# A two-layer graph network with a tensor product: node part by the tile, six gathered blocks, and another order of TensorE's work in each window

## The chip, the cores and the metric

The kernel runs on one core of one Trainium2 chip. The metric is the device time of that core in microseconds (us) from launch to end; less is better. The engines of the core are TensorE (PE; PEld is its weight load), VectorE (DVE), ScalarE (ACT), GpSimd (POOL) and SyncE (SP), each of which takes its own instructions in program order. They wait for one another through semaphores only.

## The reference

There are N = 6250 nodes with 512 features and E = 100,000 edges, sorted by destination. The destinations are drawn so that low node numbers receive far more edges than high ones. Written for what the change touches:

```python
edge_index = jnp.stack([src, dst])
h = jnp.maximum(_layernorm(x), 0)                       # 6250 x 512
# two graph layers; norm = dinv[row] * dinv[col], self loops added
h0 = layer_norm(h, g0, be0)
h  = relu(segment_sum(norm * (h0 @ W0)[row], col) + b0 + h0 @ lw0.T + lb0)
x_final = h
h1 = layer_norm(h, g1, be1)
h  = relu(segment_sum(norm * (h1 @ W1)[row], col) + b1 + h1 @ lw1.T + lb1)
x  = x + (x_final + h) @ pw.T + pb                      # x1
# tensor product on x1
h  = jnp.maximum(_layernorm(x), 0)
x0, x1 = lin(h, W_up0, W_up1)                           # 128 + 3 * 128 channels
t  = edge_attr_8                                        # E x 8
for W in (W_mlp1, W_mlp2, W_mlp3): t = 1.679177 * silu(t @ W / sqrt(W.shape[0]))
tpw = t @ W_mlp4 / 8                                    # E x 512
...                                                     # messages of x0, x1, tpw, edge_attr_4
x  = x + lin_out(segment_sum(messages, dst)) / 10
```

## The kernel before

**Tiles.** The nodes are 49 tiles of 128 rows (`NW = 49`), which are also the 49 windows of destinations of a graph layer. The edges are 784 tiles of 128 (`NT = 784`). A block is `BT = 4` edge tiles, so there are 196 blocks per layer.

**Setup.** TensorE sums the squares of the weights (line 1175), then counts edges per node by products of one-hots that VectorE makes (the histogram, line 1163). VectorE scales the weights by the squares' column norms. From the counts come the degrees, and from these each window's range of blocks.

**Node part.** For each tile: SP loads `x` (`load_x`), VectorE takes mean and variance, ScalarE and VectorE together form the first layernorm with its relu (`hrel`), then the second one (`tn`). POOL multiplies by `g0` and adds `be0` into `t32`. TensorE transposes (line 1188), ScalarE copies the transpose to `AT` (line 634), and TensorE multiplies by `W0` (line 1198) and `lw0` (line 1200). ScalarE and VectorE scale and split the product in a high and a low half (`tout`), which SP stores as a row of the table `tab_d`, and VectorE adds `b0` to the other product, which SP stores in `hl_d`. Each engine handles two tiles in turn: `norm_tiles` for tiles 2j and 2j+1, all steps of both, then `table_tiles` for the pair before. On TensorE it is `turn_tiles` for both tiles and then `project_tiles` for both. All buffers are double.

**Graph layers.** For each layer POOL gathers the table rows of the edges' sources, four indirect DMAs per block (line 549), into a ring of `NK = 4` blocks. The indices of the next block are copied ahead (line 557), and the wait for the data of the previous block, which signals `arrived`, stands after the third of the four gathers (lines 560 and 561). For each window VectorE makes one-hots of destination against node, one per visit (`onehots`, line 986). TensorE accumulates in bank 0: first the window's own rows (`tw`, line 1226, loaded by SP), then a visit (line 1233, eight matmuls) to each block that has edges of the window. A block that lies across a window boundary is visited by both windows. It is called the shared block here: the first visit of a window goes to the last block of the window before, which is still in the ring. There are 244 visits to 196 blocks in a layer. POOL may overwrite a ring slot once its block's last visit is over.

**The order of the work.** A window passes through several engines. Each engine has a list of stages with a distance d, and `peeled` runs for each w every stage of the list, in the order written, on window w - d:

```python
            with eng.Fori(depth + 1, NW) as w:
                for d, f in stages:
                    f(w - d)
```

In layer 0 the lists are

```python
peeled(ve, [(1, layer_out), (0, onehots), (2, low), (1, second_norm)])
peeled(pe, [(0, edge_sum), (1, turn), (1, dense)])
peeled(sp, [(0, load_self), (0, load_hl), (1, store_r), (2, store_tab), (2, store_hl)])
```

`layer_out(w)` (line 1010) reads bank 0 once the sum of window w is done, and frees it for window w + 1. `relu_r` makes `r`, `second_norm` with `std` and `scaled` the second layernorm in `t32`, `turn` transposes it, `copy_at` copies the transpose, `dense` multiplies by `W1` and `lw1` (lines 1266 and 1268), and `high` and `low` split the result for the table of layer 1. In layer 1 the rest of a window is `turn_xs`, `copy_xT`, `project` (line 1282), `residual`, `relu_h`, `turn_h` (line 1291), `copy_hT`, `up` and `up_out` (which SP stores, `store_up`). Beside it the radial MLP runs over two groups of 512 edges per window, which belong to no window: `load_ef`, `layer1`, `act1`, `layer2`, `act2`, `layer3`, `act3`, `store_hid` (line 424). `layer1` and `layer3` share banks 4 and 5, so that `layer1(w)` waits for `act3(w - 3)`, and `act3(w)` waits until the store of `w - 1` has landed. SP's list there is

```python
peeled(sp, [(0, load_ef), (0, load_self), (3, store_up), (0, load_hl), (4, store_hid), (0, load_r0),
            (1, load_x), (2, store_x1)])
```

The tensor product that follows gathers rows of the up table for each edge, forms the messages and scatters them.

## Time and profile before

| what | value |
|---|---|
| median of the runs | 6345.55 us (3 runs: 6323.8, 6345.55, 6354.23) |
| profiled execution | 6386.15 us, span 6383.9 us |
| mean granted clock of TensorE | 0.897 |
| busy: PE, PEld | 4974.6 us (78%), 2304.6 us |
| busy: DVE, ACT, POOL | 2858.4 us (45%), 2315.3 us (36%), 2736.9 us (43%) |
| setup | 0 to 170.5 us |
| node part | 170.5 to 797.8 us |
| layer 0 | 804.8 to 2139.5 us |
| layer 1 | 2139.5 to about 3920 us |
| tensor product | about 3920 to 6383.9 us |

The times are those of one profiled execution. A stage ends where the next one's first instructions stand. The busy share is an average over stages with different limits, so the stages have to be read by themselves. A granted clock of 1.0 is TensorE's full speed.

### The profile page before, as it was taken

The numbers are of one execution on the slowest core, as the hardware profiler recorded it, in microseconds if no ns is written. First come the engines' busy times: TensorE is split into PE (matmuls) and PEld (weight loads), VectorE is DVE, ScalarE is ACT, GpSimd is POOL, SyncE is SP. The second block draws the span as 40 slices with busy tenths as digits, with TensorE's granted clock in tenths as the row PEclk, the third lists the DMA queues.
The fourth block names the chain that finished last, engine by engine and source line by source line (L and its number), as shares of the span: only waits on it lengthen the run. The fifth ranks groups of instructions, "written<-read, shape, count | busy, mean of one in ns | idle before, by whom it ended". The sixth has DMA issues, their size and how long they took to land.

```text
span 6383.9 us, 104141 instructions
## 1 busy us (share of the span) xinstructions
PE 4974.6 (78%) x16990; PEld 2304.6 (36%) x17137; DVE 2858.4 (45%) x8231; ACT 2315.3 (36%) x6178; POOL 2736.9 (43%) x3492
## 2 busy tenths in 40 slices
PE   6566646667888556667677777999999999999998
PEld 4233312223333212223333333444444444444444
DVE  6322211233344211212222224777777777777776
ACT  0222200011111001122333335666666666666665
POOL 0211166666665565544433332444443333333332
PEclk6788867789999768888898898999999999999999
DMA  2111166667766565566655553444444434343333
GB/s 74 56 59 62 57 178 189 204 204 219 222 215 220 155 185 177 179 182 180 181 177 171 172 177 117 120 115 117 118 121 117 117 113 116 116 119 114 116 115 99
DMA packets 433670, 916.78 MB, mean 144 GB/s; under 512 B 63093, under 2 KB 170869, under 8 KB 433510
## 3 DMA queue, kind: packets, MB, share of 16 engines
q0 software_dynamic: 195840, 641.89, 34.6%
q1 hardware_dynamic: 237798, 274.56, 13.2%
q8 instruction: 9, 0.15, 0.0%
q14 instruction: 23, 0.19, 0.0%
HBM read 787.79 MB, written 128.41 MB: 144 GB/s over the span
## 4 chain that ended last, share of the span: by engine, by line
PE 35%; issue 21%; ACT 10%; DVE 9%; DVEq 7%; ACTq 4%; DMA 4%; POOL 4%; another core or an unknown queue 3%; POOLq 2%; SPq 1%
PE bank L1233 8%; PE bank L1282 4%; PE bank L1198 4%; ACT dense_w L765 4%; POOL ring L549 3%; PE bank L1363 3%; PE bank L1266 3%; PE bank L1200 3%; DVEq L1081 2%; ACT hB L754 2%; PE bank L1268 2%; DVE hA L1089 2%; DMA tw<-tab_d 2%; ACTq L751 2%
## 5 line engine op out<-in xcount | busy, mean ns | idle before, releaser
L549 POOL DMA_INDIRECT ring<-tab_d,idx x1568 | 1544.5, 985 | 1273.3 <-PE bank L1233 727.2
L1363 PE MATMUL bank<-dense_w,oh 128*128 128x512 f32 x3520 | 1618.9, 602 | 68.2 <-DVE dense_w L1098 67.3
L1233 PE MATMUL bank<-ring,ohp 128*128 x3904 | 1084.5, 435 | 483.1 <-POOLq L561 338.3
L515 POOL DMA_INDIRECT ring<-up_d,idx x880 | 881.9, 1002 | 497.3 <-POOL idx L511 348.6
L765 ACT ACTIVATE dense_w<-hA,hC 128x128 f32<-128x128 f32 x2640 | 819.9, 389 | 655.7 <-DVE hA L1089 593.5
L1363 PEld LDWEIGHTS bank<-dense_w,oh 128*128 128x128 f32 x3520 | 632.8, 190 | 859.9 <-issue 667.6
L1233 PEld LDWEIGHTS bank<-ring,ohp 128*128 x3904 | 417.0, 107 | 1126.1 <-issue 839.4
L986 DVE TENSOR_TENSOR ohp<-iota_w,dst_f 128x512 f32 x392 | 265.8, 692 | 711.3 <-PE bank L1233 333.7
L511 POOL COPY idx<-src_i 128x2 int32 x440 | 81.1, 184 | 1037.3 <-DVE dense_w L1098 964.4
L1353 PE MATMUL bank<-w,hC 64*128 64x256 f32 x3520 | 502.3, 404 | 29.0 <-issue 19.8
L1075 DVE SCALAR_TENSOR_TENSOR hA<-ring,hC,hB 128x128 f32<-128x128 f32 x880 | 270.6, 349 | 487.2 <-ACT hB L754 426.7
L1098 DVE TENSOR_TENSOR dense_w<-hA,ring 128x384 f32<-128x384 f32 x880 | 485.3, 551 | 0.0
L1353 PEld LDWEIGHTS bank<-w,hC 64*128 64x128 f32 x3520 | 308.1, 187 | 324.9 <-issue 291.3
L1198 PE MATMUL bank<-dense_w,AT 128*128 128x512 f32 x392 | 232.5, 748 | 197.6 <-ACT AT L634 197.6
L759 ACT ACTIVATE hA<-bank,hC 128x256 f32<-128x256 f32 x880 | 360.4, 458 | 20.4 <-PE bank L1353 16.3
L489 POOL TENSOR_TENSOR tn<-tn,v_g 128x512 f32<-128x512 f32 x49 | 61.1, 1269 | 645.4 <-ACT tn L626 645.4
L754 ACT ACTIVATE hB<-ring,hC 128x128 f32<-128x128 f32 x880 | 305.1, 393 | 80.7 <-issue 79.6
L719 ACT ACTIVATE hB<-bank 128x512 f32<-128x512 f32 x98 | 58.4, 597 | 696.1 <-PE bank L1327 279.8
L916 DVE RECIPROCAL mv<-mv 128x1 f32<-128x1 f32 x196 | 31.3, 160 | 623.4 <-ACT mv L665 366.8
L1083 DVE SCALAR_TENSOR_TENSOR hB<-ring,hC,hA 128x128 f32<-128x128 f32 x880 | 270.4, 349 | 34.5
L1266 PE MATMUL bank<-dense_w,AT 128*128 128x512 f32 x392 | 212.2, 691 | 63.6 <-issue 42.3
L1282 PE MATMUL bank<-dense_w,xT 128*128 128x512 f32 x392 | 254.2, 809 | 0.9 <-issue 0.9
(179 smaller groups left out, 5107.4 us busy)
## 6 DMA issues: line engine op xcount, KB each, us to landing
hC<-hid_d SPq DMA_DIRECT2D x440, 64.0 KB
tab_d<-tout SPq DMA_DIRECT2D x98, 256.0 KB, 2.0
tw<-tab_d SPq DMA_DIRECT2D x98, 256.0 KB
hlw<-hl_d SPq DMA_DIRECT2D x98, 256.0 KB
ring<-tab_d,idx POOLq DMA_INDIRECT x1568
hid_d<-hC SPq DMA_DIRECT2D x98, 256.0 KB, 4.0
hl_d<-agg SPq DMA_DIRECT2D x74, 256.0 KB, 2.1
ring<-up_d,idx POOLq DMA_INDIRECT x880
```

The lines of the kernel that those rows point to most:

```text
L515: g_.indirect_dma_start(ring_v[:, b, k, :], None, table, bass.IndirectOffsetOnAxis(idx_t[:, b, k:k + 1], 0)).then_inc(S["got"][b], 16)
L549: g_.indirect_dma_start(ring_h[:, b, k, :], None, table, bass.IndirectOffsetOnAxis(idx_b[:, b, k:k + 1], 0)).then_inc(S["got"][b], 16)
L754: ins = ac.mul(q0[:, b, k, :], ring_u[:, u, k, P:2 * P], yg[:, b, 4 * k + 1:4 * k + 2])
L759: ins = ac.mul(w13[:, k, :], w_bank[k][0][:, 0:2 * P], yg[:, b, 4 * k:4 * k + 1])
L765: ins = ac.mul(msg[:, b, k, 1, P + m * P:2 * P + m * P], t2[:, k, :], yg[:, b, 4 * k + 1 + m:4 * k + 2 + m])
L1098: ins = ve.tensor_tensor(msg[:, b, k, 0, P:].rearrange("p (m u) -> p m u", m=3), w13[:, k, P:2 * P].unsqueeze(1).broadcast_to([P, 3, P]), ...
L1198: pe.matmul(bank[2 + b][:, :], AT[:, b * 4 + i, :], W["W0"][:, i, :], start=(i == 0), stop=(i == 3))
L1233: ins = pe.matmul(bank[0][:, :], ohp_b[:, bass.ds(at, 1), k, :].rearrange("p b n -> p (b n)"), ring_b[:, bass.ds(slot, 1), k, h, :].rearra ...
L1266: pe.matmul(bank[2][:, :], AT[:, i, :], W["W1"][:, i, :], start=(i == 0), stop=(i == 3))
L1282: ins = pe.matmul(bank[2][:, :], xT[:, i, :], W["pw"][:, i, :], start=(i == 0), stop=(i == 3))
L1353: ins = pe.matmul(w_bank[k][h][:, 0:2 * P], hid[k * HID:(k + 1) * HID, b, :], w4[k * HID:(k + 1) * HID, h * 2 * P:(h + 1) * 2 * P], start= ...
L1363: ins = pe.matmul(bank[h][:, :], oh[:, b, k, :], msg[:, b, k, h, :], start=False, stop=False, skip_group_check=True)
```

## The change

It has three parts. The slots of the ring (`NK`) and of the one-hots (`NV`) are now counted apart: the ring has six blocks and the one-hots still four.

**Node part and setup.** The histogram stands before the squares on TensorE. Each engine has a list of steps with a distance in tiles, which the new function `tiles` runs tile by tile, two tiles per turn of its loop, instead of pair by pair. `before` is its wait for a double buffer. The second layernorm has its own statistics `st2` and `mv2`. On SP the store and load of the window ranges stand before the loads of `x`. Four of the biases, the histogram's one-hots and `xin` now lie in the ring's memory, so that POOL waits for the stores of `hl_d` too before the first gather.

**Gathers.** The wait for the previous block's data and its signal `arrived` stand ahead of the copy of the indices and the third gather.

**Order of a window.** `edge_sum` is cut in two: `edge_start` has the window's own rows and the visit to the shared block, `edge_rest` the visits to the new blocks. Between them stand the matmuls of older windows, in layer 0 `turn` and `dense` of window w - 2 instead of w - 1, in layer 1 the steps of windows w - 2 and w - 3. ScalarE's lists follow. The lists of SP and VectorE in both layers are unchanged.

```diff
-NK = 4
+NK = 6
+NV = 4
...
+        ring = sb("ring", [P, NK * BT * D])
         ring_h = ring[:, :].bitcast(F16).rearrange("p (b k n) -> p b k n", b=NK, k=BT)
+        for i, k in enumerate(("b0", "g0", "be0")):
+            bia[k] = ring[:, 10752 + i * D:10752 + (i + 1) * D]
+        bia["lb0"] = ring[:, 5504:5504 + D]
...
+        def tiles(eng, stages):
+            depth = max(d for d, _ in stages)
+            first = depth + depth % 2 + 2
+            def at(tile):
+                for d, f in stages:
+                    if 0 <= tile - d < NW:
+                        f(tile - d, (tile - d) // 2, (tile - d) % 2)
+            for tile in range(first):
+                at(tile)
+            with eng.Fori(first // 2, NW // 2) as j:
+                for b in range(2):
+                    for d, f in stages:
+                        f(j * 2 + (b - d), j + (b - d) // 2, (b - d) % 2)
+            for tile in range(NW - NW % 2, NW + depth):
+                at(tile)
+        def before(eng, sm, tile, back=2):
+            if not isinstance(tile, int) or tile >= back:
+                eng.wait_ge(sm, tile - (back - 1))
...
+            tiles(sp, [(0, load_x), (8, store_table)])
...
+            tiles(g_, [(0, affine)])
...
-                        visited = g_.snap(n + w + (NK + 1))
+                        visited = g_.snap(n + w + (NV + 1))
...
                             row(1)
-                            g_.tensor_copy(idx_b[:, (b + 1) % NK, :], src_i[:, bass.ds(ahead, BT)]).then_inc(S["idx_ready"], 1)
-                            row(2)
                             with g_.If(n > LAG):
                                 g_.wait_ge(S["got"][(b - LAG) % NK], landed)
                                 g_.nop().then_inc(S["arrived"], 1)
+                            g_.tensor_copy(idx_b[:, (b + 1) % NK, :], src_i[:, bass.ds(ahead, BT)]).then_inc(S["idx_ready"], 1)
+                            row(2)
                             row(3)
...
-            g_.wait_ge(t_st[0], 16 * (NW // 2 + 1))
-            g_.wait_ge(t_st[1], 16 * (NW // 2))
+            for b in range(2):
+                g_.wait_ge(t_st[b], 16 * (NW // 2 + 1 - b))
+                g_.wait_ge(hl_st[b], 16 * (NW // 2 + 1 - b))
...
+            tiles(ac, [(3, scaled1), (7, table_high), (5, copy_turned), (1, relu1), (2, std2), (0, std1)])
...
-                    peeled(ac, [(1, relu_r), (2, high), (1, std), (1, scaled), (1, copy_at)])
+                    peeled(ac, [(1, relu_r), (2, copy_at), (2, high), (1, std), (1, scaled)])
                 else:
-                    peeled(ac, [(1, act1), (1, relu_r), (2, act2), (2, std), (2, relu_h), (1, copy_xT), (3, act3),
-                                (2, copy_hT), (2, up_out), (4, lambda w: None)])
+                    peeled(ac, [(1, relu_r), (1, act1), (2, copy_xT), (3, copy_hT), (2, act2), (3, up_out), (3, act3), (2, std),
+                                (2, relu_h), (4, lambda w: None)])
 
...
+            tiles(ve, [(3, scale2), (1, scale1), (2, stats2), (7, table_low), (0, stats1)])
...
+            touch(bank[6][:, 0:NW], NW, True)
+            looped(pe, histogram, NT // 16)
+            touch(bank[6][:, 0:NW], NW, False).then_inc(deg_sum, 1)
             for L in range(2):
                 pe.wait_ge(sq_ready, L + 1)
                 for i in range(KC):
                     ins = pe.matmul(bank[7 - 2 * L][:, :], ones, wsq[:, i, :], start=(i == 0), stop=(i == KC - 1))
                 ins.then_inc(sq_sum, 1)
-            touch(bank[6][:, 0:NW], NW, True)
-            looped(pe, histogram, NT // 16)
-            touch(bank[6][:, 0:NW], NW, False).then_inc(deg_sum, 1)
             pe.wait_ge(deg_ready, 1)
...
+            def turn_tile(tile, q, b):
+                pe.wait_ge(n_g, tile + 1)
+                before(pe, n_ht, tile)
+                for i in range(4):
+                    ins = pe.transpose(bank[b][:, i * P:(i + 1) * P], t32[:, b, i * P:(i + 1) * P], ident[:, :])
+                ins.then_inc(n_tr, 1)
+            def project_tile(tile, q, b):
+                pe.wait_ge(n_ht, tile + 1)
+                before(pe, n_out, tile)
+                before(pe, n_hl, tile)
+                for i in range(4):
+                    pe.matmul(bank[2 + b][:, :], AT[:, b * 4 + i, :], W["W0"][:, i, :], start=(i == 0), stop=(i == 3))
+                for i in range(4):
+                    ins = pe.matmul(bank[4 + b][:, :], AT[:, b * 4 + i, :], W["lw0"][:, i, :], start=(i == 0),
+                                    stop=(i == 3))
+                ins.then_inc(n_mm, 1)
+            tiles(pe, [(0, turn_tile), (1, project_tile)])
...
+                def visit(slot, at, S=S, v_r=v_r):
+                    for k in range(BT):
+                        for h in range(2):
+                            ins = pe.matmul(bank[0][:, :],
+                                            ohp_b[:, bass.ds(at, 1), k, :].rearrange("p b n -> p (b n)"),
+                                            ring_b[:, bass.ds(slot, 1), k, h, :].rearrange("p b n -> p (b n)"),
+                                            start=False, stop=False, skip_group_check=True)
+                    ins.then_inc(S["used"], 1)
+                    pe.reg_add(v_r, v_r, 1)
+                def edge_start(w, S=S, c=c, v_r=v_r, visit=visit):
                     after(pe, S["y_read"], w)
                     pe.wait_ge(S["self_in"], (w + 1) * 16)
                     pe.matmul(bank[0][:, :], ident_h[:, :], tw[:, 0:D], start=True, stop=False, skip_group_check=True)
                     pe.matmul(bank[0][:, :], ident_h[:, :], tw[:, D:], start=False, stop=False,
                               skip_group_check=True).then_inc(S["self_used"], 1)
-
-                    def visit(slot, at):
-                        for k in range(BT):
-                            for h in range(2):
-                                ins = pe.matmul(bank[0][:, :],
-                                                ohp_b[:, bass.ds(at, 1), k, :].rearrange("p b n -> p (b n)"),
-                                                ring_b[:, bass.ds(slot, 1), k, h, :].rearrange("p b n -> p (b n)"),
-                                                start=False, stop=False, skip_group_check=True)
-                        ins.then_inc(S["used"], 1)
-                        pe.reg_add(v_r, v_r, 1)
-
                     if not isinstance(w, int) or w > 0:
                         v, n = pe.snap(v_r), pe.snap(c)
-                        slot, at = pe.snap((n - 1) % NK), pe.snap(v % NK)
+                        slot, at = pe.snap((n - 1) % NK), pe.snap(v % NV)
                         pe.wait_ge(S["onehot"], v)
                         visit(slot, at)
+                def edge_rest(w, S=S, c=c, v_r=v_r, visit=visit):
+                    lo, hi = block_range(pe, w)
                     with pe.Fori(lo, hi) as g:
                         v, n = pe.snap(v_r), pe.snap(c)
-                        slot, at = pe.snap(n % NK), pe.snap(v % NK)
+                        slot, at = pe.snap(n % NK), pe.snap(v % NV)
...
-                    peeled(pe, [(0, edge_sum), (1, turn), (1, dense)])
+                    peeled(pe, [(0, edge_start), (2, turn), (2, dense), (0, edge_rest)])
                 else:
-                    peeled(pe, [(2, layer2), (0, edge_sum), (1, turn_xs), (3, layer3), (2, turn_h), (1, project), (2, up),
-                                (0, layer1), (4, lambda w: None)])
+                    peeled(pe, [(0, edge_start), (2, turn_xs), (2, layer2), (3, turn_h), (2, project), (3, layer3), (3, up),
+                                (0, layer1), (0, edge_rest), (4, lambda w: None)])
```

## Rows read from the trace of the kernel before

**Rows 1.** Busy time by engine, node part (window, us, engines, clock, DMA share, GB/s)
```profile
170.50:797.80 627.30, 419.61 (x980) 191.21 (x980) 171.91 (x488) 159.62 (x293) 122.01 (x98) 0.83 0.17 60
```

**Rows 2.** TensorE's visits (line 1233) in four stretches of the two layers
```profile
804.80:1587.40 782.60, 355.54 (x1128) 128.38 (x1128) 0.79 0.66 199
1587.40:2099.70 512.30, 180.90 (x800) 78.24 (x800) 0.95 0.69 218
2323.50:2741.60 418.10, 161.62 (x512) 58.72 (x512) 0.81 0.60 179
2741.60:3895.60 1154.00, 289.88 (x1208) 119.80 (x1208) 0.89 0.58 174
```

**Rows 3.** Timeline of the node part: start, length, engine, line, count, idle before
```profile
543.61 6.44 PE L1198 MATMUL bank<-dense_w,AT 128*128 128x512 f32 x8 [8.55 <-ACT AT L634]
...
553.32 3.60 PE L1198 MATMUL bank<-dense_w,AT 128*128 128x512 f32 x8
...
560.18 1.04 PE L1188 MATMUL bank<-ident,t 128*128 128x128 f32 x8
```

**Rows 4.** Timeline of the setup; last row: the histogram's matmuls by source
```profile
24.82 0.69 DVE L840 TENSOR_TENSOR ohl<-ring 128x1024 bf16<-128x1024 bf16 x1
...
41.30 6.70 PE L1175 MATMUL bank<-ring,xT 128*128 128x512 f32 x8 [41.30 <-ACT ring L603]
...
162.51 1.27 DVE L870 TENSOR_REDUCE bound<-bank 128x1 f32<-128x512 f32 x2
...
L1163 PE MATMUL bank<-ohh,ohl x784: 267/275/301, 55.3 to 159.8; 128*128 128x49 bf16 x196
```

**Rows 5.** Timeline, one late window of layer 0
```profile
2069.75 0.38 PE L1226 MATMUL bank<-tw,ident_h 128*128 128x512 f16 x1
...
2076.41 0.75 DVE L1010 SCALAR_TENSOR_TENSOR yb<-bank,dse,hlw 128x512 f32<-128x512 f32 x1
...
2076.42 0.65 PE L1258 MATMUL bank<-ident,t 128*128 128x128 f32 x4 [0.89 <-issue]
...
2079.03 0.69 DVE L986 TENSOR_TENSOR ohp<-iota_s,dst_f 128x512 f32 x1 [0.59 <-issue]
...
2084.72 0.38 PE L1226 MATMUL bank<-tw,ident_h 128*128 128x512 f16 x1
```

**Rows 6.** Waits of POOL, 3000 to 3880 us
```profile
POOL ring L549 <- PE bank L1233: 402.9, 31, 15.7
```

**Rows 7.** Timeline of TensorE, one late window of layer 1
```profile
3793.40 0.39 PE L1226 MATMUL bank<-tw,ident_h 128*128 128x512 f16 x1 [1.78 <-DMA tw<-tab_d]
...
3806.03 1.12 PE L1291 MATMUL bank<-ident,hrel 128*128 128x128 f32 x4 [4.34 <-issue]
...
3817.82 0.39 PE L1226 MATMUL bank<-tw,ident_h 128*128 128x512 f16 x1 [1.60 <-DMA tw<-tab_d]
```

**Rows 8.** Timeline, drain at the end of layer 1
```profile
3919.93 0.60 ACT L725 ACTIVATE hC<-bank 128x512 f32<-128x512 f32 x1 [3.34 <-DMA hid_d<-hC]
```

**Rows 9.** The stores of line 424 in layer 1
```profile
DMA to landing us min/median/max: 3.8/4.0/4.3
```

**Rows 10.** Timeline, first window of layer 0
```profile
826.77 0.95 POOL L549 DMA_INDIRECT ring<-tab_d,idx  x1 [0.30 <-issue]
...
830.76 0.98 POOL L549 DMA_INDIRECT ring<-tab_d,idx  x1 [0.16 <-issue]
...
830.92 1.90 PE L1233 MATMUL bank<-ring,ohp 128*128 x8 [1.66 <-issue]
...
835.69 0.69 DVE L986 TENSOR_TENSOR ohp<-iota_w,dst_f 128x512 f32 x1 [5.13 <-remote]
836.20 1.00 POOL L549 DMA_INDIRECT ring<-tab_d,idx  x1 [3.21 <-remote]
...
837.63 3.59 PE L1233 MATMUL bank<-ring,ohp 128*128 x8 [4.81 <-POOLq L561]
```

More of the change, by code:

```diff
@@ L641, in _, with std1 @@
-            norm_tiles(0, 0, (0, 1))
-            norm_tiles(2, 1, (0, 1))
-            table_tiles(0, 0, (0, 1))
-            with ac.Fori(2, NW // 2) as j:
-                norm_tiles(j * 2, j, (0, 1))
-                table_tiles(j * 2 - 2, j - 1, (0, 1))
-            norm_tiles(NW - 1, NW // 2, (0,))
-            table_tiles(NW - 3, NW // 2 - 1, (0, 1))
-            table_tiles(NW - 1, NW // 2, (0,))
+            def std1(tile, q, b):
+                ac.wait_ge(n_st1, tile + 1)
+                ac.activation(mv[:, b, 2:3], mv[:, b, 1:2], ACT.Sqrt, bias=eps[:, 0:1]).then_inc(n_sd1, 1)
@@ new lines, in relu1, with std2, scaled1 @@
+            def relu1(tile, q, b):
+                ac.wait_ge(n_rs1, tile + 1)
+                before(ac, n_t, tile)
+                ac.activation(hrel[:, b, :], xin[:, b, :], ACT.Relu, bias=mv[:, b, 4:5], scale=mv[:, b, 3:4]).then_inc(n_h, 1)
+            def std2(tile, q, b):
+                ac.wait_ge(n_st2, tile + 1)
+                ac.activation(mv2[:, b, 2:3], mv2[:, b, 1:2], ACT.Sqrt, bias=eps[:, 0:1]).then_inc(n_sd2, 1)
+            def scaled1(tile, q, b):
+                ac.wait_ge(n_rs2, tile + 1)
+                before(ac, n_g, tile)
+                ac.activation(tn[:, b, :], hrel[:, b, :], ACT.Identity, bias=mv2[:, b, 4:5],
+                              scale=mv2[:, b, 3:4]).then_inc(n_t, 1)
@@ new lines, in copy_turned, with table_high @@
+            def copy_turned(tile, q, b):
+                ac.wait_ge(n_tr, tile + 1)
+                before(ac, n_mm, tile)
+                ac.copy(AT[:, b * 4:b * 4 + 4, :], bank[b][:, :].rearrange("p (c n) -> p c n", c=4)).then_inc(n_ht, 1)
+            def table_high(tile, q, b):
+                ac.wait_ge(n_mm, tile + 1)
+                after(ac, t_st[b], q, 16)
+                ac.mul(tout[:, b, 0:D], bank[2 + b][:, :], col(dup[:, 0, :], tile)).then_inc(n_hi, 1)
+            tiles(ac, [(3, scaled1), (7, table_high), (5, copy_turned), (1, relu1), (2, std2), (0, std1)])
@@ L943, in _, with stats1 @@
[L943 to L951 removed]
+            def stats1(tile, q, b):
+                ve.wait_ge(x_in[b], (q + 1) * 16)
+                before(ve, n_h, tile)
+                stats(xin[:, b, :], b).then_inc(n_st1, 1)
@@ new lines, in scale1, with stats2, scale2, table_low @@
+            def scale1(tile, q, b):
+                ve.wait_ge(n_sd1, tile + 1)
+                scale(b).then_inc(n_rs1, 1)
+            def stats2(tile, q, b):
+                ve.wait_ge(n_h, tile + 1)
+                before(ve, n_t, tile)
+                stats(hrel[:, b, :], b, st2, mv2).then_inc(n_st2, 1)
+            def scale2(tile, q, b):
+                ve.wait_ge(n_sd2, tile + 1)
+                scale(b, mv2).then_inc(n_rs2, 1)
+            def table_low(tile, q, b):
+                ve.wait_ge(n_hi, tile + 1)
+                ve.scalar_tensor_tensor(out=tout[:, b, D:], in0=bank[2 + b][:, :], scalar=col(dup[:, 0, :], tile),
+                                        in1=tout[:, b, 0:D], op0=ALU.mult, op1=ALU.subtract).then_inc(n_out, 1)
+                after(ve, hl_st[b], q, 16)
+                ve.tensor_tensor(hl_out[b][:, :], bank[4 + b][:, :], bia["b0"][:, :], ALU.add).then_inc(n_hl, 1)
```

172 lines of the change are left out of this document (34 added, 138 removed).

## The prediction

> **What bounds the kernel now.** I read the granted-clock column first: it is 0.83 in the node part and 0.95 and 0.89 in the later windows of the two graph layers, so TensorE pauses in all of them [rows 1, 2]. Four stretches have four different limits. In the node part TensorE sums 419.6 us of work in 627.3 us; the timeline shows a pause of 8.55 us once per pair of tiles, after which eight records take 6.44 us instead of 3.43 [rows 1, 3]. In the first windows of layer 0 POOL's gathers rule: TensorE's visits wait for them. In the later windows of layer 0 TensorE's own order rules: windows of three visits repeat in 14.97 us, with a pause of 0.89 us ahead of the transpose [rows 5]. In layer 1 it is the reverse of POOL-bound: POOL waits 402.9 us for TensorE in 880 us, since all ring slots are full, and TensorE in turn stands still 4.34 us ahead of the second transpose and 1.60 us for the window's own table rows [rows 6, 7]. The last stage, the tensor product, is untouched.
>
> **The node part.** The squares of the weights move behind the degree histogram. VectorE's first one-hots are ready at 24.8 us, so the histogram runs from about 26 us; it lasts 104.6 us (55.3 to 159.9) and ends at 130.4 [rows 4]. The squares took 13.9 us at mixed clock (41.3 to 55.2); I take 15.3, since the second half may run as slow as the first: 145.8, where VectorE read them at 162.5 before [rows 4]. That is 16.7 us less. Per tile TensorE then has two groups of eight records at 3.43 us and 0.52 us of transposes: 7.4 us at the full clock [rows 3]. The norm loop (VectorE 3.5 us of instructions per tile, ScalarE 3.3, from 171.9 and 159.6 us over 49 tiles) lies beside it [rows 1]. Program order leaves no tighter loop: the copy that a projection needs is made during the projection before it. Before the first projection five norm steps of some 4.7 us run, plus 2: 25.5 us. End after 25.5 + 48 x 7.4 + 6.9 = 387.6, plus 3 for a slow start: 390.6 in place of 627.3, 236.7 less. SP's loads and stores have two buffers and 7.4 us each. Together **-253**. Bounds: 7.4 to 7.8 us a tile, so -253 to -233.
>
> **Layer 0, new order.** The new order closes a serial loop over all engines. `edge_start(w)` waits for `layer_out(w-1)`; then come the shared visit, `turn(w-2)`, `dense(w-2)`; `low(w-2)` waits for that; in VectorE's order `second_norm(w-1)` stands behind `low(w-2)`, and `layer_out(w)` behind both. Its length from rows: `layer_out` to a ready one-hot 2.62 + 0.69 + 0.04 = 3.35 us (these were hidden behind `dense`); visit 1.83 (a third of 5.5); transpose, copy and dense 8.30; end of dense to the next `layer_out` 6.66 [rows 5]. Sum 20.14 us, for up to three new blocks, whose visits (1.8 us each) lie inside the 6.66. Against it stand 14.97 for the three-visit window and 512.3/29 = 17.7 on average in the last 29 windows [rows 2, 5]. With two new blocks the pause around the shared visit is 6.66 + 3.35 less 3.7 of visits and 0.4 of self product, 5.9 us; a visit after a pause of 4.81 us took 3.59 instead of 1.9 [rows 10], which is the lower of the clock's two levels. So 21.9 us for the 16 windows of three visits and 21.0 (half the effect) for the 13 of four (100 visits in 29 windows fix these numbers), plus 0.7 for a stall of POOL's that is told below: 644 us, **+131**. Bounds: always fast 20.14 x 29 = 584 (+72); always slow and more stalls 680 (+168).
>
> The Trainium skill (TensorE: Matmul & The Clock Gate, "Loop structure matters more than you think") says that bursts of matmuls parted by waits run cold; by that rule all shared visits of both layers would be slow, 12 and 36 us more than I take, and the sum would be near 6330, inside the forecast's own range. No row has the split pause (self product in its middle) that decides between them.
>
> The first 19 windows of layer 0 (123 new blocks in 782.6 us) are POOL's [rows 2]. A block takes 5.1 us to issue, plus 3.2 us of stall after every 16 gathers: 5.9 us [rows 10]. Six ring blocks take nothing from that. The wait for landed data moves ahead of the index copy and the third row. The data of a block are in 4.15 us after its fourth row began (826.77 to 830.92); the third row of the next begins after 3.99 now, so the wait costs nothing there. Moved ahead of the copy, it delays each block by 0.45 to 0.8 us, where no stall has drained the queue: I take 0.3 a block on average, 123 x 0.3 = +37, and give 29 back for TensorE waits that go: **+8** (-30 to +60).
>
> **Layer 1.** Here a transfer enters the loop. `act3(w-3)` waits until `store_hid(w-4)` has landed; SP has it behind `store_up(w-3)`, and that now waits for `up_out(w-3)` of the same window (it was a window older before). `layer1(w)` waits for `act3(w-3)`, since both use the same banks, and the new blocks come behind `layer1(w)`. Length: 3.35 as above; visit 1.83; TensorE's own work: a window of three visits lasted 24.42 us, less pauses of 4.34 and 1.60, less 5.5 for visits, 0.44 for the self rows, 1.6 for the slow clock and 1.9 for `layer1`, is 9.1, plus 0.9 because `act1` and the copy of the transpose now follow `layer2`: 10.0 [rows 7]. Then `up_out` 0.7; from its end to `act3` 3.34 in the drain at the end of the layer [rows 8], plus 0.56 for `load_hl`, which stands between the two stores, 3.9; in the stream the store took 4.0 to land instead of 2.9, 5.0 [rows 9]; I take 4.5. `act3` and `layer1` after some 6 us of pause, so slow: 4.0; closing 0.4. Sum 24.85 + 1.85 a new block; +0.9 for half a slow shared visit, +0.4 for stalls: 26.15. The last 40 windows have 151 visits, 111 of them new: 40 x 26.15 + 205 = 1251 against 1154: **+97** (bounds: all fast with 3.9: +21; all slow with 5.0 and two stalls in three windows: +160). The eight windows before them have 56 new blocks: POOL 353 us at 6.3, the loop 8 x 26.15 + 104 = 313; each window takes the longer one: 360 against 418.1, **-58** [rows 2]. Here the order gains: half of POOL's waits vanish, because up to six blocks are gathered during the loop. First window +8. Layer 1 **+47**.
>
> The Trainium skill (DMA: Bandwidth & Descriptors, "Anatomy of one DMA") gives a transfer about 2.0 us plus bytes over 436 GB/s, by which the 256 KB store would take 2.6 us; the rows have 2.9 to 4.0. By that rule layer 1 would lose some 35 us less and the sum would be near 6245.
>
> **Sum.** -253 + 131 + 8 + 47 = -67 us on the profiled execution's 6386.15 = 6319; the median of the runs is 0.9936 of that execution, so **6280 us**, -1.0%. A measurement of this kernel tells about 0.5% (32 us) from no change.
>
> **Rivals.**
> 1. The loops run at their floor: clock high, store in 2.9 us. Layers +72, +21, -65; sum -225: 6120 us. For it: pauses split by a short self product may keep the clock (a visit after 1.66 us took 1.90 [rows 10]). Against: in layer 1 4.34 us of pause slowed what followed to 1.12 us. 25%.
> 2. Slower: POOL's stall hits the loops in full. After every 16 gathers POOL stands 3.2 us, and VectorE with it (its one-hot at 835.69 came after 5.13 us of "remote"; POOL's row [rows 10]). The 69 TensorE-ruled windows hold 182 blocks, 46 stalls; at 3.2 us that is 147 instead of the 36 in my sum, +111: 6389 us. It turns the sign at 2.2 us a stall. Against: part of them falls beside matmuls. 20%.
> 3. The node part doesn't reach TensorE's rate (a hop of ScalarE or SP stays in the loop at 9 us a tile): +78, 6356 us. Against: no order of waits that I found. 10%.
> **Chances.** Forecast 45% (6200 to 6360), rivals 25, 20 and 10%. Faster by over 0.5%: 34 + 25 + 0 = 59%; within: 7 + 2 + 8 = 17%; slower: 24%. Eight in ten: 6120 to 6420.
>
> **What would show it.** In the node part: clock 1.0, tiles 7.4 us apart, no wait for ACT AT. In layer 0's late windows: TensorE standing 3 to 6 us ahead of each shared visit, waiting for VectorE, windows of 20 to 23 us. In layer 1: ScalarE's third activation waiting for the hid store, `layer1` waiting for it, windows near 30 us with two new blocks; POOL still waiting for TensorE there. POOL: a gap of 0.5 us more ahead of the index copy. Wrong if VectorE's norm or the store of hid isn't what ends these waits, or if the first 19 windows of layer 0 change by more than 60 us.

## The result and the profile after

The changed kernel takes 6501.49 us (median of 4 runs, 6473.35 to 6512.83) against 6343.68: ratio 1.0246, 95% interval 1.0204 to 1.0288. It is slower by 2.5%. The forecast was 1.0% faster, 6280 us, and its widest range ended at 6420. The profiled execution took 6473.35 us, span 6471.5, granted clock 0.885.

Busy time by stretch, kernel after (window, us, PE, PEld, DVE, ACT, POOL, clock, DMA share, GB/s): node part, windows 0 to 18 and 19 to 47 of layer 0, windows 1 to 8 and 9 to 47 of layer 1.

```profile
170.50:533.60 363.10, 356.14 (x969) 166.50 (x967) 164.10 (x463) 145.18 (x275) 116.78 (x93) 0.99 0.29 102
533.60:1297.30 763.70, 515.31 (x1525) 200.08 (x1526) 186.31 (x339) 53.02 (x89) 520.04 (x641) 0.77 0.67 201
1297.30:1950.50 653.20, 485.54 (x1467) 204.28 (x1467) 214.18 (x419) 87.17 (x145) 301.73 (x388) 0.85 0.57 174
2183.20:2571.80 388.60, 253.25 (x776) 102.83 (x777) 76.94 (x141) 66.74 (x99) 236.92 (x294) 0.78 0.64 194
2571.80:3931.50 1359.70, 948.70 (x2706) 404.65 (x2706) 273.32 (x537) 366.32 (x545) 459.90 (x582) 0.80 0.49 146
```

The visits alone (line 1212), windows 19 to 47 of layer 0 and 9 to 47 of layer 1; the last line is the kernel before (line 1233) over windows 9 to 47 of layer 1:

```profile
1297.30:1950.50 653.20, 228.95 (x800) 87.69 (x800) 0.85 0.57 174
2571.80:3931.50 1359.70, 402.27 (x1184) 142.34 (x1184) 0.80 0.49 146
...
2741.60:3865.60 1124.00, 284.42 (x1184) 117.47 (x1184) 0.89 0.59 176
```

Against [rows 1] the node part lost its pauses: TensorE is busy for 356 of 363 us. Against [rows 2] the late windows grew from 512.3 to 653.2 us in layer 0 and, up to the start of window 48, from 1124.0 to 1359.7 in layer 1. There the same 1184 matmuls of the visits take 402 us in place of 284, and the stretch has a clock of 0.80 in place of 0.89. ([rows 2] gives 290 us and 1208 matmuls because its stretch runs on to 3895.6 us.)

The node part on TensorE's timeline, the answer to [rows 3]:

```profile
344.27 0.60 PE L1183 MATMUL bank<-ident,t 128*128 128x128 f32 x4
344.71 3.60 PE L1191 MATMUL bank<-dense_w,AT 128*128 128x512 f32 x8
348.15 3.60 PE L1193 MATMUL bank<-dense_w,AT 128*128 128x512 f32 x8
351.58 0.60 PE L1183 MATMUL bank<-ident,t 128*128 128x128 f32 x4
```

A tile takes 7.31 us (344.27 to 351.58), without a pause. The squares, now behind the histogram, start at 131.3 us. One late window of layer 0, TensorE with the VectorE steps that close its loop, the answer to [rows 5]:

```profile
1859.88 0.39 PE L1222 MATMUL bank<-tw,ident_h 128*128 128x512 f16 x1 [3.68 <-DVE yb L1007]
...
1862.60 3.59 PE L1212 MATMUL bank<-ring,ohp 128*128 x8 [2.12 <-DVE ohp L983]
...
1871.33 3.60 PE L1256 MATMUL bank<-dense_w,AT 128*128 128x512 f32 x8
...
1874.76 3.62 PE L1212 MATMUL bank<-ring,ohp 128*128 x16
...
1875.98 0.75 DVE L1023 SCALAR_TENSOR_TENSOR tout<-bank,dup,tout 128x512 f16<-128x512 f32 x1 [12.15 <-ACT tout L684]
...
1880.60 0.74 DVE L1019 TENSOR_TENSOR t<-t,v_be 128x512 f32<-128x512 f32 x1
...
1881.39 0.75 DVE L1007 SCALAR_TENSOR_TENSOR yb<-bank,dse,hlw 128x512 f32<-128x512 f32 x1
```

This is the loop of the forecast: `dense` ends at 1874.9, `low`, the norm and `layer_out` follow one another on VectorE, and TensorE stands still twice, for 3.68 us ahead of the window's own rows and for 2.12 us ahead of the shared visit. The shared visit takes 3.59 us, the two new ones 1.8 each. One late window of layer 1, TensorE, and then ScalarE's third activation in it, the answer to [rows 7, 8]:

```profile
3361.94 0.39 PE L1222 MATMUL bank<-tw,ident_h 128*128 128x512 f16 x1 [1.23 <-DVE yb L1007]
...
3364.77 2.36 PE L1212 MATMUL bank<-ring,ohp 128*128 x8 [2.23 <-DVE ohp L983]
...
3376.99 1.05 PE L1285 MATMUL bank<-wup,hT 128*128 128x128 f32 x8
3383.81 3.77 PE L1296 MATMUL bank<-ef,w 16*128 16x512 f32 x4 [5.77 <-ACT hC L727]
3387.52 8.23 PE L1212 MATMUL bank<-ring,ohp 128*128 x24
```

```profile
3383.16 0.60 ACT L727 ACTIVATE hC<-bank 128x512 f32<-128x512 f32 x1 [4.42 <-DMA hid_d<-hC]
```

ScalarE waits 4.42 us for the store of the hidden activations, and TensorE waits 5.77 us for ScalarE. Then the three new visits take 8.23 us, 2.7 each. POOL's wait for TensorE, as in [rows 6], 3000 to 3900 us (us in total, times, longest):

```profile
POOL ring L559 <- PE bank L1212: 519.4, 38, 22.1
```

**Where the time went.** Stage lengths in us, from the start of the window's own rows (line 1226 before, 1222 after) in each trace. The runs fell on several chips. The kernel before took about 6190 us on some, about 6380 on others and 6344 on the first, so comparisons are made within a kind: "A" are the first traces, "B" chips where before takes about 6190, "C" where it takes about 6380.

| stage | before A | after A | before B | after B | before C | after C |
|---|---|---|---|---|---|---|
| to layer 0 | 804.8 | 533.6 | 803.6 | 531.8 | 804.7 | 531.5 |
| layer 0, 0 to 18 | 782.5 | 763.7 | 717.5 | 771.0 | 782.7 | 780.9 |
| 19 to 47 | 512.3 | 653.2 | 469.3 | 647.2 | 508.2 | 655.0 |
| 48 and drain | 39.8 | 56.5 | 40.9 | 58.1 | 40.0 | 58.2 |
| layer 1, 0 | 184.0 | 176.1 | 162.1 | 177.5 | 181.9 | 177.4 |
| 1 to 8 | 418.1 | 388.6 | 396.6 | 388.8 | 417.2 | 398.7 |
| 9 to 47 | 1124.0 | 1359.7 | 1072.8 | 1355.6 | 1126.3 | 1365.6 |
| 48 and drain | 62.2 | 82.5 | 62.4 | 86.5 | 62.3 | 87.3 |
| tensor product | 2456 | 2457 | 2454 | 2457 | 2455 | 2458 |

(before B and C: c3_before, c2_before; after B and C: c5_changed, c4_changed.)

### The profile page after: what moved, and what is told of

Read it like the earlier page. It is cut to its first block, busy times and chain, and to the rows that moved or that the text cites. A ratio compares the mean times of both kernels' runs of the same rounds, so it can differ in the third digit from the quotient of the medians.

```text
span 6471.5 us, 104993 instructions
## 1 busy us (share of the span) xinstructions
PE 5116.0 (79%) x17136; PEld 2325.7 (36%) x17137; DVE 2861.4 (44%) x8231; ACT 2324.4 (36%) x6178; POOL 2728.4 (42%) x3492
## 4 chain that ended last, share of the span: by engine, by line
PE 33%; issue 23%; DVE 10%; ACT 8%; DVEq 8%; DMA 5%; ACTq 5%; POOL 4%; SPq 1%; POOLq 1%; another core or an unknown queue 0%
PE bank L1212 9%; POOL ring L559 3%; PE bank L1351 3%; PE bank L1296 3%; PE bank L1191 3%; PE bank L1193 3%; DMA hid_d<-hC 3%; DVEq L1078 3%; ACT hB L756 2%; PE bank L1270 2%; ACT dense_w L767 2%; DMA ring<-tab_d,idx 2%; ACTq L753 2%; PE bank L1254 2%; DVE hA L1086 2%
## 5 line engine op out<-in xcount | busy, mean ns | idle before, releaser
L1212 PE MATMUL bank<-ring,ohp 128*128 x3904 | 1253.1, 489 | 485.4 <-issue 184.4
L1212 PEld LDWEIGHTS bank<-ring,ohp 128*128 x3904 | 452.6, 117 | 1316.1 <-issue 1094.7
L663 ACT ACTIVATE r<-yb 128x512 f32<-128x512 f32 x98 | 61.7, 630 | 1038.7 <-DVE yb L1007 612.1
L1296 PE MATMUL bank<-ef,w 16*128 16x512 f32 x196 | 180.4, 1070 | 286.6 <-ACT hC L727 286.6
L1007 DVE SCALAR_TENSOR_TENSOR yb<-bank,dse,hlw 128x512 f32<-128x512 f32 x98 | 73.5, 750 | 556.6 <-PE bank L1155 465.2
L1094 DVE TENSOR_TENSOR dense_w<-hA,ring 128x128 f32<-128x128 f32 x880 | 249.3, 283 | 0.0
L1023 DVE SCALAR_TENSOR_TENSOR tout<-bank,dup,tout 128x512 f16<-128x512 f32 x49 | 36.8, 750 | 465.2 <-ACT tout L684 371.2
L1090 DVE TENSOR_TENSOR dense_w<-hB,bank 128x128 f32<-128x128 f32 x880 | 213.1, 284 | 40.6
```

Of the source, the lines that this page charges most:

```text
L1212: ins = pe.matmul(bank[0][:, :], ohp_b[:, bass.ds(at, 1), k, :].rearrange("p b n -> p (b n)"), ring_b[:, bass.ds(slot, 1), k, h, :].rearra ...
L1296: pe.matmul(bank[4 + b][:, :], w1[:, :], ef[:, b, :], start=True, stop=True).then_inc(m1, 1)
```

## The experiments

**The two kernels again (c1_changed, c4_changed, c5_changed, c2_before, c3_before).** No edit.

> The changed kernel again, beside the others of this call on one chip. On the first chip it was 1.0246 times the time of before; on a chip where before takes 6188 us in place of 6344 the ratio may differ, since what differs between the chips is the clock of TensorE in the layers: if the changed order pauses on every chip, its ratio there is higher, 1.04 to 1.05; if both gain alike, 1.025.

> The kernel before again, for its trace on the chip of this call. Expected: node part, setup and tensor product within 1% of the first trace, and any difference in the graph layers alone, where the granted clock was 0.8 to 0.95.

> The kernel before, for its trace on the chip of this call. Question: the first window of layer 0 (29 blocks, POOL alone rules) took 180 us with 6 or 7 stalls of POOL of over 3 us in both traces of before, and 162 to 163 us with none in the two kernels that kept the old place of the wait and got the new node part, on another chip. If the stalls belong to the chip, this trace has them or not as its chip's other runs have; if they belong to the old kernel's layout, it has them whatever the chip.

> The changed kernel beside the others of this call. If this chip's kernel before takes about 6190 us (a chip without stalls of POOL), the traces so far give 6480 to 6500 us, a ratio of 1.045 to 1.05; if about 6380 us, 1.02 to 1.025 as in the two comparisons so far.

> The changed kernel again. On a chip where before takes about 6190 us: 6480 to 6500 us, ratio 1.045 to 1.05, since the moved wait holds every block to 6.15 us where the old place allows 5.6 there. On one where it takes about 6380: 1.02 again.

Measured: c1 1.0209 (1.018 to 1.0239) and c4 1.0189 (1.017 to 1.0207) where before takes 6383 and 6381 us; c5 1.0456 (1.0438 to 1.0473) where it takes 6193. Before itself differs between the chips by 190 us, nearly all in the layers; the changed kernel by 44.

**e1_node_only and e2_node_ring6 (B).** e1 has the new node part and setup alone, e2 has them with the ring of six. `edge_sum` stays cut in two in both, but its halves stand next to each other:

```diff
-peeled(pe, [(0, edge_start), (2, turn), (2, dense), (0, edge_rest)])
+peeled(pe, [(0, edge_start), (0, edge_rest), (1, turn), (1, dense)])
...
-NK = 6
+NK = 4
```

(layer 1 and ScalarE back to before's lists, the wait for landed data at its old place; the last two lines in e1 only).

> The new node part and setup alone: ring of four, old place of the wait for landed data, old orders on TensorE and ScalarE in both layers. By the two traces the node part and setup ended 271 us earlier in the changed kernel and nothing in it should depend on the layers: 6345 - 271 = about 6075 us (6050 to 6100), with the layers as long as before (1335 and 1782 us to the first product of the tensor stage). Rival: part of the gain is lent by the new layer orders or the larger ring, or the layers start worse after a faster front: above 6110 us.

> As the run before, with six ring blocks used in place of four. Theory: in the long first windows POOL's own issue rules and in the later ones TensorE does, so two more blocks only move the place at which POOL waits: within 20 us of the run with four. Rival: blocks gathered ahead feed the windows of medium length (4 to 18 of layer 0, 1 to 8 of layer 1), where neither rules for long: 20 to 60 us less.

Measured 0.9645 (0.9629 to 0.9661), 215 us less than before, not the 271 expected, and 0.9542 (0.9526 to 0.9558). Front 531.2 us as in the change; about 50 of the missing us are in windows 9 to 47 of layer 1 (1125.0 against 1072.8). The ring gives 68 us, above the 20 of my theory. By the traces it is 391.6 to 348.0 us in windows 1 to 8 of layer 1 and 1125.0 to 1085.0 behind them. TensorE in e1, 2900 us:

```profile
2884.13 1.90 PE L1213 MATMUL bank<-ring,ohp 128*128 x8
2887.69 3.85 PE L1213 MATMUL bank<-ring,ohp 128*128 x16 [1.67 <-issue]
```

Cutting `edge_sum` in two put the reading of the block range between the shared visit and the others, and in this order that makes a pause of 1.67 us.

**e7_whole, e8_whole_landed (B), e6_landed (C).** e7 is e2 with `edge_sum` in one piece, the range read first; e8 is e7, and e6 is e2, with the wait for landed data at its new place.

```diff
-def edge_start(w, ...):
+def edge_sum(w, ...):
+    lo, hi = block_range(pe, w)
...
-def edge_rest(w, ...):
-    lo, hi = block_range(pe, w)
```

> New node part, ring of six, old orders and old place of the wait for landed data, and edge_sum in one piece again: the reading of the block range into registers stands ahead of the window's first product, not between the shared visit and the others. In the trace of the kernel with the ring of six that reading made a pause of 1.6 us between them. Theory: the pause goes where TensorE rules, some 48 windows of layer 1 and 15 of layer 0 by 1.6 us less the slack: 50 to 100 us less, ratio to before about 0.94 to 0.945. Rival: the pause is cover for a wait that comes later (the turned h, the table rows): ratio 0.95 to 0.955.

> As e7_whole, with the wait for landed data ahead of the index copy and the third gather. By the first windows of the runs so far (5.6 us a block with the old place, 6.15 with the new, on one chip) the new place costs 0.55 us a block where POOL rules: 28 + 28 blocks of the two first windows and up to 95 + 56 of the next ones, 30 to 110 us more than e7_whole. Rival: on a chip on which POOL runs into stalls with the old place, the new one costs nothing: within 15 us.

> Node part and ring of six as in the earlier run with the old orders, with one edit more: the wait for landed data and its signal ahead of the index copy and the third gather, as in the change. My sum had 0.3 us more per block where POOL rules: about 37 us more in the first 19 windows of layer 0 and 20 in windows 1 to 8 of layer 1. Rival: the earlier signal frees TensorE as much as it holds POOL: within 15 us of the run without it, or less.

Measured: e7 0.9424 (0.9408 to 0.944), windows 9 to 47 of layer 1 from 1085.0 to 1032.1: the cut cost 53 us there. e8 0.9624 (0.9608 to 0.964): the moved wait costs 123 us on this chip, more than the 30 to 110 expected, 67 of them in the first 19 windows of layer 0 and none in windows 9 to 47 of layer 1 (1030.4 us). e6 0.9565 (0.954 to 0.9589) on a C chip: its first 19 windows take 782.4 us, as before's 782.7 there, but windows 9 to 47 of layer 1 take 1176.8, 92 more than e2's on B. The first of e7, then e8, POOL in the first window:

```profile
603.85 0.98 POOL L559 DMA_INDIRECT ring<-tab_d,idx  x1 [0.16 <-DMA ring<-tab_d,idx]
...
608.93 0.98 POOL L559 DMA_INDIRECT ring<-tab_d,idx  x1 [0.16 <-DMA ring<-tab_d,idx]
```

```profile
602.90 0.97 POOL L559 DMA_INDIRECT ring<-tab_d,idx  x1 [0.50 <-issue]
...
608.12 0.18 POOL L570 COPY idx<-src_i 128x4 int32 x1 [0.40 <-DMA ring<-tab_d,idx]
608.80 0.97 POOL L559 DMA_INDIRECT ring<-tab_d,idx  x1 [0.50 <-issue]
```

From one third gather to the next it is 5.08 us with the old place and 5.90 with the new: 0.40 ahead of the copy and 0.34 more behind it. The whole window divided by its 29 blocks gives 5.63 and 6.15 us a block.

**e3_hid_first (B).** The changed kernel; on SP in layer 1

```diff
-[(0, load_ef), (0, load_self), (3, store_up), (0, load_hl), (4, store_hid), ...
+[(0, load_ef), (0, load_self), (4, store_hid), (3, store_up), (0, load_hl), ...
```

> The changed kernel with one edit: in layer 1 SP issues the store of the hidden activations of window w-4 ahead of the up store of w-3, not behind it. Store theory: the third activation no longer waits 4.8 us for the transfer, TensorE's pause goes, layer 1's first product (3.8 us) and the new blocks' visits (2.6 us) return to the full clock (1.9 and 1.8 us): windows 9 to 47 fall from 34.9 to about 26 us, 300 to 350 us less in all, 6150 to 6200 us. Rival 1: the pause goes but the clock stays low for another reason: 39 x 4.8 = 187 us less, 6310. Rival 2: another wait takes its place (residual, r0, the up store): less than 60 us, above 6440.

Measured 1.0003 (0.9993 to 1.0013), against 1.0456 for the changed kernel on B: 282 us less, where 300 to 350 were expected. Windows 9 to 47 fall from 1355.6 to 1107.1 us. TensorE:

```profile
3215.08 1.98 PE L1296 MATMUL bank<-ef,w 16*128 16x512 f32 x4 [1.25 <-ACT hC L727]
3217.99 7.03 PE L1212 MATMUL bank<-ring,ohp 128*128 x24 [0.93 <-issue]
```

The pause of 5.8 us ahead of `layer1` is 1.25, and `layer1` is back at 1.98. But a pause of 0.93 us now shows ahead of the new visits, for the reading of the block range, and a new visit still takes 2.38 us on average.

**e4_filled (B) and e11_filled_twice (C).** The changed kernel with products of zeros added to bank 0 (the sums stay): e4 24 ahead of `layer1`; e11 26 there and 9 ahead of the shared visit.

```diff
-(0, layer1), (0, edge_rest), (4, lambda w: None)])
+(0, keep), (0, layer1), (0, edge_rest), (4, lambda w: None)])
```

> The changed kernel with 24 products of zeros added to bank 0 between up and layer1 of each window of layer 1 (about 5.2 us of TensorE work inside its pause of 5.7 us; the sums are unchanged). The wait for the store stays. Clock theory: layer1 and the new visits behind the pause run at the full clock, 1.9 less for the one and 0.8 for each of 2.8 visits, 4.1 us a window, 160 us in 39 windows: about 6340 us. Rival: those visits are slow for another reason (traffic of the gathers on the ring): no change, 6480 to 6520 us.

> The changed kernel with products of zeros in two pauses: 9 (2 us) ahead of the shared visit in both layers, 26 (5.8 us) ahead of layer1. Clock theory: the shared visits of layer 0 fall from 3.3 to about 1.9 us and the new visits of layer 1 from 2.6 to about 1.8: windows of layer 0 from 22.5 to 21.1, of layer 1 from 35 to 31: 200 us less in all. Rival: visits are held by something that filling doesn't touch (weights or rows read while the gathers write): shared visit above 3 us, new visits above 2.4.

Measured: e4 1.0398 (1.0381 to 1.0415), windows 9 to 47 1302.6 us, 53 less than the changed kernel's on B, a third of what I expected. e11 1.0141 (1.0117 to 1.0165), 31 us less than c4, where 200 were expected. In layer 0 the shared visit falls from 3.34 to 1.86 us and the late windows from 655.0 to 627.8. In layer 1 the pause ahead of `layer1` falls from 6.3 to 0.6 us, `layer1` from 3.8 to 2.4, the matmuls of new visits that start over 0.35 us behind the one before from 11 to 7.5 a window, and a new visit from 2.62 to 2.36 us. So most of the slow shared visit comes from the pause ahead of it; of the slow new visits only a part comes from the long pause ahead of `layer1`. Two windows of e11, one behind the other:

```profile
3392.81 5.31 PE L1212 MATMUL bank<-ring,ohp 128*128 x16 [0.98 <-issue]
...
3419.69 2.39 PE L1298 MATMUL bank<-ef,w 16*128 16x512 f32 x4
3423.11 5.68 PE L1212 MATMUL bank<-ring,ohp 128*128 x24 [1.04 <-issue]
```

The granted clock over the same visits (window, us, PE, PEld, clock, DMA share, GB/s), then over the two visits of e1 shown above, which stand behind a pause of 1.67 us:

```profile
3392.81:3397.95 5.14, 5.14 (x16) 1.98 (x16) 0.67 0.24 58
3423.11:3428.63 5.52, 5.52 (x24) 2.33 (x24) 1.00 0.16 53
...
2887.60:2891.60 4.00, 3.79 (x16) 1.55 (x16) 1.00 0.85 278
```

Two visits at a clock of 0.67 take 5.31 us, three at 1.00 take 5.68. Over windows 9 to 47 of e11, 291 matmuls of new visits start over 0.35 us behind the one before, and 279 of them stand where the granted clock is 0.5; in the changed kernel (first trace) it is 437 of 437. So what slows the new visits is the lower clock and not the gathers' traffic. The mean clock over the new visits is 0.67 in the changed kernel, 0.74 in e3, 0.79 in e4, 0.77 in e11 and 1.00 in e2. The reading of the range does not explain the rest by itself: in e2 it makes 30 pauses of 1.3 to 1.8 us ahead of the same visits, and a new visit takes 1.91 us.

**e5_norm_first and e10_norm_both (C).** The changed kernel, layer 0; e5 the first edit, e10 both:

```diff
-peeled(ve, [(1, layer_out), (0, onehots), (2, low), (1, second_norm)])
+peeled(ve, [(1, layer_out), (0, onehots), (1, second_norm), (2, low)])
...
-peeled(ac, [(1, relu_r), (2, copy_at), (2, high), (1, std), (1, scaled)])
+peeled(ac, [(1, relu_r), (2, copy_at), (1, std), (1, scaled), (2, high)])
```

> The changed kernel with the last two stages of VectorE's list in layer 0 exchanged: second_norm(w-1) before low(w-2). Loop theory: 4.6 us of norm leave the way from the end of dense to the next layer_out, but 4.8 us of visits and closing lie beside it, so that layer_out comes 1.6 to 1.9 us earlier: windows 19 to 47 fall from 22.5 to about 20.8 us, 45 to 55 us in all. Rival: TensorE is held by something else there (clock, visits), and the windows stay within 0.5 us of 22.5.

> The changed kernel with second_norm(w-1) ahead of low(w-2) on VectorE and std(w-1), scaled(w-1) ahead of high(w-2) on ScalarE, layer 0 only. Loop theory: the norm now runs beside dense, layer_out follows the closing of the sum, windows 19 to 47 fall from 22.5 to about 20.8 us, 45 to 55 us in all, ratio to the changed kernel 0.992. Rival: TensorE then waits for the window's own table rows, whose load stands on SP behind the stores of low's results: no more than 15 us less, or more time than before.

Measured: e5 1.0358 (1.0333 to 1.0383), late windows 746.6 us, 92 more than c1 on the same chip, where about 50 less were expected: my expectation had forgotten ScalarE. VectorE in e5:

```profile
1887.23 0.16 DVE L918 RECIPROCAL mv<-mv 128x1 f32<-128x1 f32 x1 [17.77 <-ACT mv L667]
```

The norm moved ahead of `low`, but its `std` stood behind `high`, which waits for `dense`. With both moved (e10) the ratio is 1.0109 (1.0086 to 1.0132) and the late windows take 597.2 us, 20.6 each: the loop is the one that the forecast named.

**e12_healed (C).** The changed kernel with e3's, e10's and the old place's edits.

> The changed kernel with three things mended: the hidden store first on SP, the norm ahead of high and low in layer 0, the wait for landed data at its old place. Theory (the order itself costs a pause at the head of each window, for the freed bank and the shared one-hot, and slow visits behind it): still 150 to 250 us above the kernel with the old orders and ring of six (0.942 to 0.954 of before on a chip without stalls), a ratio of 0.97 to 0.99. Rival: the three mended waits were the whole loss: ratio at or below 0.955.

Measured 0.9826 (0.9803 to 0.985), 6274.68 us: as expected. e6, on another C chip, has the old order, the ring of six, the cut `edge_sum` and even the moved wait, and takes 6106.84. POOL in its first window, on a C chip:

```profile
560.54 0.95 POOL L559 DMA_INDIRECT ring<-tab_d,idx  x1 [0.30 <-issue]
564.83 0.94 POOL L559 DMA_INDIRECT ring<-tab_d,idx  x1 [3.33 <-PE bank L1212]
```

The profile names a visit as what ended the wait of 3.33 us. That visit ran from 559.16 for 3.51 us and had ended 2.2 us before POOL went on, so it is not what held it. This is the stall of [rows 10], back with the old place of the wait.

**e9_layer1 and e13_layer1_again (B, B).** e7 and four moves of stages in layer 1, on three engines:

```diff
-peeled(sp, [(0, load_ef), (0, load_self), ...
+peeled(sp, [(0, load_self), (0, load_ef), ...
-peeled(pe, [(2, layer2), (0, edge_sum), (1, turn_xs), (3, layer3), (2, turn_h), (1, project),
-            (2, up), (0, layer1), ...
+peeled(pe, [(2, layer2), (0, edge_sum), (1, turn_xs), (3, layer3), (1, project), (2, turn_h),
+            (0, layer1), (2, up), ...
-peeled(ac, [(1, act1), (1, relu_r), (2, act2), (2, std), (2, relu_h), (1, copy_xT), ...
+peeled(ac, [(1, act1), (1, relu_r), (1, copy_xT), (2, act2), (2, std), (2, relu_h), ...
```

> As e7_whole, with three moves in layer 1: SP loads the window's table rows ahead of the edge features (TensorE stood 1.6 us a window for them), TensorE projects w-1 before it transposes h of w-2 (it stood 3.6 us for ScalarE's h there), layer1 stands ahead of up, and ScalarE copies the transpose of xs ahead of its norm steps. Theory: up to 1.6 + 2.9 us in each of 40 windows, 120 to 180 us less than e7_whole. Rival: the waits come back at the next step (the copy of the transpose, bank 2 read by the residual): less than 60 us.

> The kernel of e9_layer1 again. On a chip without stalls of POOL 0.91 again; on one with them the first windows of both layers give nothing back, so that the saving is some 270 us of front, 25 to 70 of the ring, 170 to 230 of layer 1: 5830 to 5900 us of 6380, 0.915 to 0.925.

Measured 0.9105 (0.909 to 0.9121) and 0.9103 (0.9088 to 0.9119), 5637.48 and 5635.11 us, both on B chips; on a C chip it was not run. e9 takes 196 us less than e7, a little more than the 120 to 180 expected. Windows 9 to 47 fall from 1032.1 to 854.4 us. TensorE in e9:

```profile
2923.00 5.34 PE L1212 MATMUL bank<-ring,ohp 128*128 x24
...
2934.40 0.67 PE L1277 MATMUL bank<-ident,hrel 128*128 128x128 f32 x4 [0.25 <-ACT hrel L694]
2936.31 1.98 PE L1294 MATMUL bank<-ef,w 16*128 16x512 f32 x4 [1.24 <-ACT hC L727]
```

Nothing is left of the 1.60 us ahead of the own rows and 0.25 of the 3.64 to 4.34 ahead of the second transpose, and these three visits take 1.78 us each. The four moves were not run apart.

## Why the prediction was wrong

**Node part, -253:** right. -271.2 in the traces. A tile takes 7.31 us (7.4), and the squares ended at about 145.9 us (145.8). Rival 3 is out.

**Layer 0, windows 19 to 47, +131:** right, +140.9. The loop is shown by e10, which takes its norm out: 2.0 us a window less, 1.7 expected. That the size fits is in part luck. I had put in 0.7 us a window for POOL's stalls, and none came. Against that, the way from the `turn` to the end of `dense` took 9.0 us (8.30), and all shared visits ran slow (3.31 us on average), where I had taken half the effect for 13 of the 29 windows. The rule of the Trainium skill (TensorE: Matmul & The Clock Gate, "Loop structure matters more than you think"), that matmuls parted by long waits run cold, was the better guide here; e11 shows it for the shared visit. In layer 1 the shared visits took 2.79 us on average, close to my half (1.83 + 0.9).

**Layer 0, first windows, +8:** -18.8 in the first pair, but +53.5 on B and -1.8 on C. The moved wait costs 0.5 us a block where POOL rules (6.15 against 5.63), not 0.3; and it takes away the stalls that [rows 10] show. In before's first window on C POOL lost 21 us in 6 gaps of over 3 us between gathers; in the changed kernel there are none; with the old place put back (e12) there are 6 again, of 2.8 to 4.3 us. I had added the stall to both sides as a fixed price. On a chip with these stalls the move costs nothing: layer 0 of e12 (old place) and e10 (new place), equal there but for that and run on one C chip, takes 789.5 and 775.2 us up to window 18, 602.9 and 597.2 behind it. On B it costs 123 us in all (e8 against e7).

**Layer 1, windows 1 to 8, -58:** -29.5. I gave the gain to the order. By the runs on B the ring gives 44 us (e1 to e2), the moved wait takes 19 back (349.2 to 368.1, e7 to e8), and the store's loop takes 30 (388.8 against 358.6 in e3). What is left for the order itself is 10 (368.1 to 358.6, e8 to e3).

**Layer 1, windows 9 to 48, +97:** this step failed. Windows 9 to 47 alone lost 235.7 us. The mechanism, the store's transfer in the loop, was right: e3 takes the store out of the loop and 248 us with it. The term that was mis-sized is "1.85 a new block". By parts, means over 39 windows of the trace after, us:

| part | forecast | measured |
|---|---|---|
| `layer_out` to shared visit | 3.35 | 3.77 |
| shared visit | 1.83 + 0.9 | 2.79 |
| own work up to `up` | 10.0 | 10.50 |
| `up_out` | 0.7 | 0.72 |
| to `act3` | 4.5 | 4.85 |
| `act3`, `layer1` | 4.0 | 4.36 |
| 2.79 new visits | 5.2 | 7.34 |
| closing | 0.4 | 0.61 |
| POOL's stalls | 0.4 | in the above |
| window | 31.3 | 34.93 |

The window is 3.6 us longer than forecast, and 2.2 of it are in the new visits: 2.63 us each in place of 1.85. I let the slow clock end with `layer1`; in the trace it goes on through 11 matmuls of the new visits. The rest is small terms of up to 0.5 us each. Even my upper bound, +160, held the new visits at 1.85. The parts of my sum add up to 24.78 and not 24.85, which is 3 us over 40 windows. The section that I cited for the store (DMA: Bandwidth & Descriptors, "Anatomy of one DMA", in the Trainium skill) gives its figures for transfers that GpSimd issues, while SP issues this one. The way from the end of `up_out` over the store to `act3`, which I had put at 4.5 us, took 4.85.

**The two drains:** not in the sum. Stages at a distance of 2 and 3 windows instead of 1 and 2 run on behind the last window: +16.7 and +20.3 us.

**Sum.** By terms, forecast and first traces: -253 and -271, +8 and -19, +131 and +141, +47 and +198 (-8, -30, +236), drains 0 and +37, tensor product 0 and +1: -67 and +88. Of the 155 us between, about 140 are windows 9 to 47 of layer 1. Rival 2 ended on the right side for a wrong reason: in the changed kernel POOL had no such stalls in the first 19 windows of layer 0, and most of the loss beyond the forecast came from the clock over the new visits. The profiled execution before was 0.7% above its median and the one after 0.4% below, so the medians differ by 158 us where the traces differ by 88; that rest is not explained by stages.

**Still open:** why the clock stays at its lower level over 7.5 matmuls of new visits a window when the long pauses are filled. A pause of 0.93 us remains ahead of them, but e2 has longer ones there and visits at the full clock behind them; a kernel in the new order without that pause was not run.

## What to carry to other kernels

A stage order for one engine is a loop over all: follow it through the lists of the engines that stay as they are (here SP's store behind a store, VectorE's norm behind `low`), and when such a loop has a pause, price at the lower clock more than the next instruction (here `layer1` and 11 matmuls behind it). Of the three parts of this change the front alone took off 271 us, 4.3% of before, and the ring about 1%; the new order and the moved wait gave back more than both, and only runs of the parts could tell. Pauses that a trace shows at a known place (a load behind a wait on SP, a transpose ahead of its input) gave 3.2% of before by four moves of stages. The new order, with its three worst waits mended, was still slower than the old one (6274.68 against 6106.84 us on C chips).

## What the hardware showed that was not expected

The kernel before takes 6178 to 6203 us on some chips and 6365 to 6392 on others (6324 to 6354 in the first runs), with the tensor product equal within 2 us. In the first window of layer 0 POOL has 6 gaps of 2.8 to 4.3 us between gathers on the slower ones (180 us or more for 29 blocks) and none on the others (162 to 164 us). With the wait for landed data after the second gather in place of the third, no chip has them there, and all take 177 to 180 us.

POOL is not the only engine concerned, and the moved wait does not cure it all. In e6, which has the moved wait and ran on a C chip, ScalarE's second activation starts 2 to 4.6 us after its last input was ready in 12 of the 39 windows 9 to 47 of layer 1; in e2, e7 and e8, on B chips, it never starts more than 0.04 us after. The kernel before has 3 to 5 such delays, of up to 3.2 us, in its traces A and C and none in B. One of e6's:

```profile
2837.93 1.88 PE L1315 MATMUL bank<-hB,w 128*128 128x512 f32 x4
...
2844.25 0.60 ACT L721 ACTIVATE hB<-bank 128x512 f32<-128x512 f32 x1 [16.86 <-remote]
```

That activation waits for products of TensorE alone, the last of which ended at 2839.8. What limit it is that POOL and ScalarE meet there was not found.
